# A two-layer graph network on one core: four rooms for quarters of a weight chunk, each loaded by its own condition, and the sums in another order

## The reference

```python
def _sage_sum(h, src, dst, Ws, Wn, b):
    h_neigh = jax.ops.segment_sum(h[src], dst, num_segments=N_NODES)
    return h @ Ws + h_neigh @ Wn + b
h0 = relu(layernorm(x))
h1 = _sage_sum(h0, src, dst, Ws1, Wn1, b1)
out = x + _sage_sum(h1, src, dst, Ws2, Wn2, b2)
```

## Time and profile before

| | us |
|---|---|
| profiled execution, its own time | 655.63 |
| its span | 653.8 |
| median of three timed runs | 656.73 |
| TensorE busy (PE) | 640.9 |
| GpSimd busy (POOL) | 210.3 |
| ScalarE busy (ACT) | 174.3 |
| VectorE busy (DVE) | 286.0 |

### The profile page before, as it was taken

One profiled execution on the slowest core, in us unless ns is written; L12 is line 12 of the kernel. 1 busy time (PEld: TensorE's weight loads), 2 busy tenths in 40 slices (PEclk: granted clock), 3 DMA queues, 4 the chain that ended last, 5 costly groups with the idle time before them and its releaser, 6 DMA issues.

```text
span 653.8 us, 8550 instructions
## 1 busy us (share of the span) xinstructions
PE 640.9 (98%) x3304; PEld 556.3 (85%) x3304; DVE 286.0 (44%) x392; ACT 174.3 (27%) x292; POOL 210.3 (32%) x198
## 2 busy tenths in 40 slices
PE   7999989999999999999999999999999999999997
PEld 5788778887899989999999988888888888887885
DVE  6763898871112111210022483325387987611111
ACT  5454243222123222313233122211334333100000
POOL 6224352000256666576580158003214012000000
PEclk9999999999999999999999999999999999999999
DMA  8622321003165676466754686444322242011111
GB/s 299 213 53 43 94 90 49 33 34 128 57 216 201 209 237 246 143 227 239 257 224 163 230 259 218 154 145 155 126 82 81 72 157 95 32 65 49 61 48 63
DMA packets 62726, 90.63 MB, mean 139 GB/s; under 512 B 16546, under 2 KB 34988, under 8 KB 62679
## 3 DMA queue, kind: packets, MB, share of 16 engines
q1 hardware_dynamic: 42342, 76.08, 34.6%
q10 hardware_dynamic: 20336, 13.91, 6.8%
HBM read 58.49 MB, written 31.48 MB: 138 GB/s over the span
## 4 chain that ended last, share of the span: by engine, by line
PE 62%; DMA 1%; DVE 0%; issue 0%; ACT 0%; POOL 0%; SPq 0%; DVEq 0%
PE PS L1274 29%; PE PS L1290 14%; PE PS L1237 10%; PE PS L1245 9%; DMA quarters<-ws_in 1%; DVE W_st L1021 0%; POOL prep_sum L624 0%; ACT W_st L750 0%; DVE s L1089 0%; ACT prep L801 0%; SPq L493 0%; DVEq L1088 0%
## 5 line engine op out<-in xcount | busy, mean ns | idle before, releaser
L1274 PE MATMUL PS<-right,left 128*128 128x512 f32 x840 | 190.6, 389 | 0.0
L1274 PEld LDWEIGHTS PS<-right,left 128*128 128x128 f32 x840 | 157.7, 188 | 32.7
L1109 PE MATMUL PS<-W,HT 128*128 128x512 f32 (+1 forms) x456 | 114.7, 399 | 2.7 <-ACT y_out L674 1.8
L1237 PE MATMUL PS<-HT,W_st 128*128 128x416 f32 (+1 forms) x576 | 110.7, 352 | 2.4 <-DVE W_st L1021 1.4
L1237 PEld LDWEIGHTS PS<-HT,W_st 128*128 128x128 f32 x576 | 107.9, 188 | 4.4 <-issue 3.4
L1109 PEld LDWEIGHTS PS<-W,HT 128*128 128x128 f32 (+1 forms) x456 | 81.3, 185 | 21.3 <-ACT y_out L674 2.9
L1245 PE MATMUL PS<-AT,y_st 128*128 128x416 f32 (+2 forms) x480 | 92.2, 351 | 0.0
L1245 PEld LDWEIGHTS PS<-AT,y_st 128*128 128x128 f32 (+1 forms) x480 | 90.1, 188 | 0.8
L657 POOL TENSOR_TENSOR left_sum<-h1T 128x640 f32<-128x640 f32 x24 | 41.9, 1747 | 150.2 <-PE PS L1274 119.9
L624 POOL TENSOR_TENSOR prep_sum<-quarters 128x512 f32<-128x512 f32 x40 | 52.7, 1320 | 100.0 <-PE PS L1109 62.8
L1290 PE MATMUL PS<-y_high,AT 128*128 128x512 f32 (+1 forms) x200 | 78.3, 392 | 0.0
(11 more groups left out here) (96 smaller groups left out, 476.9 us busy)
## 6 DMA issues: line engine op xcount, KB each, us to landing
sums_dram<-prep SPq DMA_DIRECT2D x40, 512.0 KB, 2.9
right<-sums_dram SPq DMA_DIRECT2D x40, 512.0 KB, 3.5
y_dram<-y_out ACTq DMA_DIRECT2D x18, 256.0 KB, 2.0
y_st_raw<-y_dram ACTq DMA_DIRECT2D x8, 576.0 KB
s<-x_in SPq DMA_DIRECT2D x18, 256.0 KB
out<-s SPq DMA_DIRECT2D x18, 256.0 KB
xin<-x_in SPq DMA_DIRECT2D x8, 512.0 KB, 11.6
W_raw<-wn_in SPq DMA_DIRECT2D x16, 256.0 KB, 5.1
```

Source lines behind the costliest of these rows:

```text
L1109: ins = nc.tensor.matmul(PS[:r, bank, :], HT[:, a, k, t * P:t * P + r], W[:, k, b, :], start=first and m == 0, stop=last and m == 2)
L1237: ins = nc.tensor.matmul(PS[:, banks[c], 0:w_], W_st[:, a, k, :], HT[:, b, k, o_:o_ + w_], start=k == 0 and m == 0, stop=False)
L1274: ins = nc.tensor.matmul(PS[:, BANKS2[g % 8], :], left[:, k, a, i * P:(i + 1) * P], right[:, KB - 1 - k, b, :], start=k == 0 and j == 0, s ...
```

## The change

The rooms hold other blocks and the five sums of a chunk come in another order. A new function free_at gives, for each room, the number of sums of a chunk after which no later one reads it: 2, 4, 5 and 5. Each quarter has a load of its own, which waits for so many sums of the chunk before, and stands in SyncE's order ahead of the store of the chunk's sum number max(free_at - 3, 0): 0, 1, 2 and 2. The constant LOAD_AT goes.

```diff
-QUARTERS = ((0, 0), (1, 1), (0, 1), (1, 0))
-SUMS = (1, 3, 6, 4, 7)
+QUARTERS = ((1, 0), (0, 0), (1, 1), (0, 1))
+SUMS = (4, 7, 1, 6, 3)
-LOAD_AT = 2
+def free_at(q):
+    return max(i for i, m in enumerate(SUMS) if QUARTERS[q] in RIGHT[m][:2]) + 1
-            def load_quarters(batch):
+            def load_quarter(batch, q):
                 what, k = BATCHES[batch]
                 if batch:
-                    sp.wait_ge(prep_summed, batch * len(SUMS))
-                for q, (row, col) in enumerate(QUARTERS):
-                    quarter(what, row, col, k, quarters[:, q, :]).then_inc(quarter_in[q], 16)
-            load_quarters(0)
+                    sp.wait_ge(prep_summed, (batch - 1) * len(SUMS) + free_at(q))
+                quarter(what, *QUARTERS[q], k, quarters[:, q, :]).then_inc(quarter_in[q], 16)
+            for q in range(len(QUARTERS)):
+                load_quarter(0, q)
             def store_sums(part):
                 for i in prepared(part):
+                    batch, n = divmod(i, len(SUMS))
+                    for q in range(len(QUARTERS)):
+                        if max(free_at(q) - 3, 0) == n and batch + 1 < len(BATCHES):
+                            load_quarter(batch + 1, q)
                     sp.wait_ge(prep_lo, i + 1)
                     sp.dma_start(sums_dram[i, :, :, :], ...)
-                    batch, q = divmod(i, len(SUMS))
-                    if q == LOAD_AT and batch + 1 < len(BATCHES):
-                        load_quarters(batch + 1)
```

## The result

The changed kernel takes 653.56 us (median of 22 runs), the kernel before, beside it, 655.16 us (22 runs). The ratio is 0.9967 with a 95% interval of 0.9951 to 0.9983: 2.2 us less, between 1.1 and 3.2. So the change makes the kernel faster by a little over what can be told from nothing. I had forecast a gain of 1.55 us and given "faster" 0.41 against 0.54 for "no change".

The account below looks back on a forecast made before the run. TensorE was taken as the bound, busy 640.9 of 653.8 us, with one stall at feature tile 3. Timed median 656.73 - 1.55 = 655.2, set at 655.0 as the stall may be somewhat longer; range 653.3 to 656.8.

Parts of the forecast that it names:

- The place and the mechanism: Start of feature tile 3: TensorE waits for W_st, queued on ScalarE behind a sum with late quarters; 1.55 us.
- sum 15: First sum of chunk 3 on GpSimd: predicted to end at 233.9 us, at worst 236.1.
- the preparation: GpSimd's forty sums and their parts: still ends near 340 us, since ScalarE's parts pace it.
- SyncE's new waits: Quarter loads ahead of stores in SyncE's order: cost taken as 0, between 0 and 1 us off the path.
- idle time for quarters: GpSimd's idle time before L624, five to six us at each chunk: shrinks to under 2 us a chunk.
- a tile with no disturbance: Table of feature-tile stretches: 25.04 us taken as undisturbed, giving the loss 1.54 + 0.40 - 0.39 = 1.55 us.
- 2.8 us to spare in every tile: VectorE's low part of W_st: ready 22.2 us into a tile of 25.04.
- under 7 us in every tile: Landing time of the y_st load in the changed kernel; more than 9 us would make D right.
- rival B: Stall goes and was larger in ordinary executions, at tile 3 and nearly so at tile 5: 654; chance 0.27.
- A: The stall at tile 3 goes at the size seen, 1.55 us: 655.0; chance 0.55.
- C: No change: the wait only changes hands, or the gain is lost at the first products: 656.7; chance 0.13.
- D: Slower: y_st's load, sharing the transfer with quarters, lands 2.5 us late in two tiles: 660.2; chance 0.05.

Follow-up runs that it names:

- e1: Kernel before with the changed loads but the old order of sums and rooms; ratio 0.9955 (653.65 us).
- e3: Kernel before with ScalarE's high part of W_st put ahead of the three sums of part 2j + 1; ratio 0.9939 (653.38 us).
- r1_after: Changed kernel profiled once more, nothing altered; its stage from tile 0 to the first of the products took 197.29 us.
- e2: Kernel before with the new order of sums and rooms but the old loads; ratio 1.0012 (657.39 us).
- r1_before: Kernel before profiled once more, nothing altered; stage 202.00 us, with waits of 1.1 us at tile 3 and 1.6 at tile 5.
- e4: Changed kernel with ScalarE's high part of W_st put ahead of the three sums of part 2j + 1; ratio to the kernel before 0.9969 (654.22 us).
- e7: Changed kernel with GpSimd made to wait for VectorE's low part of W_st before certain sums; ratio to the kernel before 0.9948 (652.9 us).

## Why the prediction came out as it did

The place and the mechanism were right. The wait at tile 3 was for the quarters of sum 15, it is gone in four of four profiles, and e1 shows that the loads did it; e3 removed it without touching the loads. The single starts were near: sum 15 ended at 233.7 (233.9 predicted, in an execution whose tile 2 ended 0.9 us later), the preparation at 336.9 us. SyncE's new waits cost nothing: GpSimd waited at most 1.6 us for a store, in stretches where it was ahead anyway. Its idle time for quarters fell from 30.8 us to 2.9 (the 6.0 us ahead of sum 15 in the kernel before, which the profile puts down to "issue", not counted).

The step that failed is the first one, the reading of the table of stretches: I called 25.04 us "a tile with no disturbance" and booked tile 4's 24.65 as 0.39 us won back. 24.65 is the tile at the fast step, and 25.04 at the slow one. A stage without a wait takes 200.34 us at the slow step (e3) and 197.29 at the fast one (r1_after). For the execution at hand the 1.55 was right, as its tiles 0 to 2 were at the slow step already and the wait had no fast step to break; for others it was too small. (The window of tile 3 also ended 0.16 us late: by the products' starts tile 3 took 25.28 and tile 4 24.73, which changes the sum by under 0.1.) The wait costs its own 1.1 to 1.7 us, and as a rule 0.38 us more in each of the five tiles behind it, when it breaks the fast step. Over the profiles: the stage takes 201.6 us in the mean before and 198.65 after, 3.0 less. The waits make up 1.2 of it (2.0 in the mean before, 0.7 after), the pace 1.7, of which 0.4 is the slow start of the first profile and lies behind no wait. With three and four profiles that split is rough, and what sets the pace stays open. The timed gain, 2.2 us, lies between my 1.55 and these 3.0, and its interval holds both. So the term is mis-sized by some 0.6 us (1.4 by the profiles), which happened to lie on the bound: I had 0.3% as "no change", and it measured 0.33%.

The second step that failed is "2.8 us to spare in every tile". It took the low part of W_st as 1.23 to 1.95 us long, from the spread in the earlier trace rows. In the changed kernel it took 6 us at tile 5 in three of four profiles and cost 0.5 to 1.3 us there, and W_st's load landed in up to 7.6 us, not 4.8, so that even without a hold-up 0.9 us were left at tile 2 of r1_after. y_st, for which I had named under 7 us in every tile, landed in 7.0 to 7.9 us in 8 of 32. The better fed GpSimd is the likely cause of the 6 us, which none of the 24 low parts in three profiles of the kernel before took; e2, with the old loads, shows that it can happen without it. So the change gives part of its gain back. The Trainium skill, "SBUF — State Buffer", section "Who interferes with whom", says that a VectorE instruction with two inputs in SBUF contends with a GpSimd instruction that reads SBUF, and that the second to issue blocks until the first is done. The traces agree (1.23 us alone, 1.95 beside one instruction; 1.30 us for GpSimd alone, 2.28 beside VectorE), and go beyond it: the one that waits isn't sure to be next, it was passed over three times. What decides whether it gets in, as in r1_after, or not stays open.

That the measured 653.56 us lies nearest to rival B's 654 says little, as both B and A started from 656.73 us, the median of three runs, and 22 runs of the kernel before gave 655.16. By the gain, 2.2 us lies between A (1.55) and B (some 2.7). B's reason, a larger stall in ordinary executions, is borne out at tile 5 alone, where r1_before shows the 1.6 us it spoke of. C fell: the wait at tile 3 is gone, and nothing is lost behind the stage (285.9 us before and after). D did not come about here, and e4 shows that it can.

## What to carry to other kernels

Before calling a repeated stretch "undisturbed", list all its values: two close clusters are two states, and what a change gains depends on which of them it leaves the kernel in. A wait on the bounding engine can cost more than its length, so price what runs behind it too. When an engine is fed better, look for whom it can hold up: its gaps may have been somebody's turn. When a remedy works in one profile, look whether it had anything to do there: in e7 the added wait held nothing up where it mattered. And where a late input holds up another because both stand in one engine's order, turning the two round (e3, one line) can do as much as making the input early.

## What the runs showed of the hardware that was not expected

- The 128 x 128 by 416-column matmuls start 186.8, 189.6 or 191.0 ns apart at the full clock, in long unbroken runs. The step changed mostly at waits: behind 8 of 9 waits that met the fast step it was 189.6 or 191.0, and so it was behind 13 of 15 that met a slow one.
- VectorE's 128 x 1024 subtraction took 1.23 us alone, some 1.95 (up to 2.4) beside one GpSimd instruction, and 5.6 to 6.2 us once in each of five of sixteen profiles, while GpSimd's instructions followed one another without a gap. Such runs stood beside many low parts that took no longer than 2.4 us, so a run alone does not hold VectorE out.
- At 83 to 86 us TensorE waited 1.1 to 2.0 us for ScalarE (y_out, L679 in the changed kernel) in all sixteen profiles. Behind that wait the granted clock fell from 2.4 to 1.2 GHz for 3.4 us in five of them (waits of 1.83 to 1.97 us) and stayed up in the others, two of which waited 1.89 and 1.91 us. Such a fall makes a span longer by some 1.7 us, an estimate (half of 3.4).
